# Second block of a two-block window-attention kernel: exponentials divided by their sums before they are turned, scores and mixes in one lump each, keys spread by transfers

## The chip, the cores and the metric

One core of a Trainium2 chip runs the whole program. The metric is the device time of one launch in microseconds (us). Every kernel computes in float32, with some products split into a high and a low part.

## The reference, cut to what matters

The input is 32 images of 56 x 56 pixels with 96 channels. Block 0 is a shifted 7 x 7 window attention with 12 heads of 8 channels and an MLP; the change doesn't touch it. Block 1 is this, with 8 x 8 windows and 6 heads of 16 channels:

```
xn = layernorm(x) * g1 + b1
windows = 8 x 8 windows of xn              # 32 * 49 = 1568 windows of 64 tokens
q, k, v = windows @ w_qkv + b_qkv          # 6 heads of 16; q is scaled by 1/4
attn = softmax(q @ k^T, axis=-1)           # exp(s - max) / sum, per query and head
out = attn @ v                             # per head
x = x + (out @ w_proj + b_proj)
h = gelu(layernorm(x) @ w_fc1 + b_fc1) @ w_fc2 + b_fc2    # 96 -> 384 -> 96
result = x + h
```

## The kernel before, in words

The program is two blocks one after the other, `swin_block` (names `swin_...` in the profile) and `plain_block` (names `plain_...`), with an array in DRAM between them. Only `plain_block` is changed.

It works in groups of 8 windows, which are 4 pairs (128 tokens each), so 196 groups. Nothing schedules the work but the order in which it is written: each engine has a `body(g, phase)` with a list of steps, and `run_groups` calls it for every `g`. A step carries an offset: `residual(-2, A)` in body `g` works on group `g - 2`. So a group passes through several bodies, and in each body the engines work on up to eight different groups. The main part is a hardware loop with 36 bodies in one turn. Steps are held together by counting semaphores, whose names are in the table `STEPS`; every step waits for its inputs and for the last reader of the buffer that it overwrites. The `x1` buffer is single, and so `residual` (VectorE, writes `x1`) waits for `x1_norm` and `x1_res` of the group before, both written by GpSimd.

What one group needs, with the engine:

- SyncE: four transfers of 48 KB load the windows (`load`, L1147), four store the result (`store`, L1154). A load may start when `x_res` and `x_norm` of two groups before are made.
- VectorE: mean and variance (`partial_x`, `moments_x`), GpSimd: their power -1/2, centring and scaling (`power_x`, `norm_x`), and `residual_x`, the input plus a constant row.
- TensorE turns the tokens (`turn_x`), ScalarE copies them twice (`copy_x`, `high_x`), and VectorE takes the difference of the two copies (`low_x`, L1505: both its inputs are in SBUF).
- TensorE makes keys, queries and values. VectorE adds the biases (`bias_k`, `bias_q`). GpSimd spreads the keys over two head columns by a multiplication with a 0/1 mask (`spread_keys`, L1548, two halves).
- TensorE: scores in two halves of two pairs (`scores`, L1195). VectorE: greatest score and difference (`shift`, once per pair). ScalarE: exponentials. TensorE turns them key-major (`turn_probs`), ScalarE copies them (`copy_turned`).
- TensorE: exponentials times values, and with a matrix of ones their sums, in two halves (`mix`, L1209). ScalarE: logarithm of the sums and exponential of its negative (`log_totals`, `invert_totals`). VectorE: product of the two (`normalise`).
- TensorE: projection. VectorE: first residual (`residual`), moments (`partial_x1`, `moments_x1`). GpSimd: `power_x1`, `norm_x1`, and `residual_x1` (writes `x1_res`). TensorE turns it, makes three chunks of the hidden layer (`hidden`), ScalarE GELU, TensorE `output`, VectorE `result`.

GpSimd's body before is:

```
residual_x(1); power_x(2); spread_keys(1, 0); spread_keys(1, 1)
norm_x(2); residual_x1(-2); power_x1(-2); norm_x1(-2)
```

Of the kernel before, what the change touches and what calls it, by code (L numbers as in the profile page):

```python
# [40 lines left out]
PAIRS = 4  # L41
# [15 lines left out]
class Plain:  # L57
# [18 lines left out]
    "reciprocal": "1 / sum of a group's first two pairs in the second block",  # L76
    "q_hat": "queries ready for the scores", "k_hat": "keys ready to be spread over heads",
    "k_heads": "two pairs' keys spread over heads",
# [3 lines left out]
    "prob": "exponentials",  # L82
# [879 lines left out]
def plain_block(nc, cfg, src, dst, par, const, psum):  # L962
# [14 lines left out]
    with ctx:  # L977

        def sb(name, shape, dtype=F32):
            return ctx.enter_context(nc.sbuf_tensor(f'{cfg.name}_{name}', shape, dtype))  # L980
# [22 lines left out]
        head_mask = sb('head_mask', [DIM, J])  # L1003
# [5 lines left out]
        sum_heads = sb('sum_heads', [128, HB, 32])  # L1009
# [15 lines left out]
        inv_total = sb('inv_total', [DIM, 2, 2 * TT])  # L1025
# [22 lines left out]
        with setup:  # L1048
# [13 lines left out]
            loads += [(ident[:, :], const['ident']), (w_fc1[:, :], par['fc1_w']), (w_fc2[:, :, :], par['fc2_w'].rearrange('(c p) n -> p c n', p=128)), (w_qkv[0:DIM, :], par['qkv_w']), (w_proj[0:DIM, :], par['proj_w']), (b_qk[:, :], par['qkv_b'][0:2 * DIM].rearrange('(t c) -> c t', t=2)), (b_v[:, :], column(par['qkv_b'][2 * DIM:3 * DIM])), (b_fc1[:, :], par['fc1_b'].rearrange('(c p) -> p c', p=128)), (row_fc2[:, :], every_row(par['fc2_b'], DIM)), (head_mask[:, :], const[f'{cfg.name}_head_mask']), (sum_heads[:, :, :], const[f'{cfg.name}_sum_heads'])]  # L1062
# [69 lines left out]
        def earlier_half(g, h):  # L1132
            return (g, 0) if h else (g - 1, 1)
        with nc.Block() as block:
# [4 lines left out]
            def _(sp):  # L1139
# [13 lines left out]

                def store(n, parity):  # L1154
# [4 lines left out]
                for n in range(8):  # L1159
                    load(n, n % 2)  # L1160
                with sp.Fori(4, groups // 2) as m:
# [3 lines left out]
                for n in range(groups, groups + 2):  # L1165
                    store(n - 8, n % 2)
# [6 lines left out]
            def _(pe):  # L1173

                def body(g, phase):
# [9 lines left out]
                    def all_windows(first):  # L1185
                        part, pair, column = [list(d) for d in first.ap]
                        return bass.AP(first.tensor, first.offset, [part, pair, [HALF, 2], column])

# [489 lines left out]
```

## Time and profile before

| | us |
|---|---|
| median of 3 runs | 7353.15 (7351.54 to 7354.21) |
| the profiled execution | 7355.68 |
| its span | 7353.9 |
| PE busy | 7179.3 (98%) |
| ACT busy | 6373.4 (87%) |
| DVE busy | 5991.6 (81%) |
| POOL busy | 5233.9 (71%) |

PE is TensorE, DVE is VectorE, ACT is ScalarE, POOL is GpSimd, and SPq is the queue on which SyncE issues transfers. The first block takes until about 4440 us of the span, the second the rest. A busy share is an average over the whole span: how much of it one group of the second block takes is read from the order of time.

### The profile page before, as it was taken

The page shows a single profiled execution, that of the slowest core. Times are in us where ns is not written, and L with a number is a line of the kernel's source. Part 1 is how long each engine was busy: PE and PEld are TensorE (multiplying, and loading weights), DVE is VectorE, ACT ScalarE, POOL GpSimd, SP SyncE. Part 2 cuts the span into 40 slices and gives each one's busy share as a digit, 9 for nine tenths or more (in the row PEclk, how much of TensorE's full clock was granted, in tenths as well). Part 3 has the DMA queues.
Part 4 walks back from the last instruction along what each step waited for, and adds up shares of the span by engine and source line. Part 5 has one row for each costly group of instructions (what it writes and reads, how often), then busy time and mean ns, then how long its engine had stood idle before and what let it go on. Part 6 is the DMA issues. An engine that isn't in the chain of part 4 may idle for free. (4 is left out here: it accounts for less than half of the span.)

```text
span 7353.9 us, 317113 instructions
## 1 busy us (share of the span) xinstructions
PE 7179.3 (98%) x113246; PEld 5509.1 (75%) x113246; DVE 5991.6 (81%) x12718; ACT 6373.4 (87%) x12032; POOL 5233.9 (71%) x5957
## 2 busy tenths in 40 slices
PE   6999999999999999999999996999999999999999
PEld 4777777777777777777777775777777777777777
DVE  5888888888888888888888885777777777777776
ACT  5999999999999999989999986887887887887887
POOL 3777777777777777777777775666666666666665
PEclk9999999999999999999999998999999999999999
DMA  0111111111111111111111101111111111111111
GB/s 21 30 30 30 29 30 30 29 29 31 30 30 29 30 30 30 29 29 30 29 30 29 30 25 24 30 30 29 30 30 29 30 30 29 30 30 29 30 30 26
DMA packets 342624, 214.39 MB, mean 29 GB/s; under 512 B 265624, under 2 KB 341144, under 8 KB 341144
## 3 DMA queue, kind: packets, MB, share of 16 engines
q1 hardware_dynamic: 341146, 194.49, 10.7%
q8 instruction: 951, 15.58, 0.9%
q14 instruction: 527, 4.32, 0.2%
HBM read 78.66 MB, written 77.07 MB: 21 GB/s over the span
## 5 line engine op out<-in xcount | busy, mean ns | idle before, releaser
L881 POOL TENSOR_TENSOR swin_score<-swin_score,swin_top 113x588 f32<-113x588 f32 x1024 | 1203.1, 1175 | 743.6 <-DVE swin_top L753 743.2
L624 ACT ACTIVATE swin_probT<-swin_ps_probs 128x339 f32<-128x339 f32 x2048 | 922.1, 450 | 199.2 <-PE swin_ps_probs L481 178.2
L1553 POOL TENSOR_TENSOR plain_k_heads<-plain_k_hat,plain_head_mask 96x512 f32<-96x512 f32 x392 | 398.9, 1037 | 897.1 <-DVE plain_k_hat L1444 897.1
L481 PE MATMUL swin_ps_probs<-swin_ident,swin_prob 113*128 113x113 f32 x6144 | 991.1, 270 | 7.0 <-ACT swin_probT L624 7.0
L481 PEld LDWEIGHTS swin_ps_probs<-swin_ident,swin_prob 113*128 113x128 f32 x6144 | 667.7, 141 | 355.6 <-issue 321.5
L748 DVE TENSOR_TENSOR swin_score<-swin_ps_scores,swin_bias_tab 113x588 f32<-113x588 f32 x1024 | 777.1, 759 | 174.1 <-PE swin_ps_scores L471 172.9
L753 DVE TENSOR_REDUCE swin_top<-swin_score 113x12 f32<-113x588 f32 x1024 | 769.0, 751 | 0.2
L630 ACT ACTIVATE swin_prob<-swin_score 113x588 f32<-113x588 f32 x1024 | 719.1, 702 | 5.8 <-POOL swin_score L881 2.9
L1431 DVE TENSOR_REDUCE plain_top<-plain_ps_scores 128x6 f32<-128x384 f32 x784 | 432.7, 552 | 263.0 <-PE plain_ps_scores L1206 263.0
L784 DVE SCALAR_TENSOR_TENSOR swin_x<-swin_y,swin_y_rstd,swin_x_res 98x96 f32<-98x96 f32 x1024 | 601.1, 644 | 0.8 <-POOL swin_y_rstd L899 0.7
L495 PEld LDWEIGHTS swin_ps_mixed<-swin_probT,swin_v_heads 128*32 128x32 f32 x24576 | 422.3, 109 | 222.2 <-issue 146.0
L471 PE MATMUL swin_ps_scores<-swin_k_heads,swin_q_hat 32*64 32x196 f32 (+1 forms) x12288 | 577.7, 347 | 4.8 <-DVE swin_score L748 4.8
L564 PE MATMUL swin_ps_dense<-swin_w_fc,swin_hid 128*98 128x96 f32 x6144 | 578.8, 251 | 1.2 <-ACT swin_hid L701 1.2
L1332 ACT ACTIVATE plain_probT<-plain_ps_probs 128x384 f32<-128x384 f32 x784 | 382.2, 488 | 221.1 <-PE plain_ps_probs L1230 220.9
L495 PE MATMUL swin_ps_mixed<-swin_probT,swin_v_heads 128*32 128x49 f32 x24576 | 563.0, 210 | 2.1 <-ACT swin_probT L624 1.0
L564 PEld LDWEIGHTS swin_ps_dense<-swin_w_fc,swin_hid 128*98 128x98 f32 x6144 | 560.8, 168 | 1.5 <-ACT swin_hid L701 1.5
L1271 PE MATMUL plain_ps_dense<-plain_w_fc,plain_hid 128*128 128x96 f32 x4704 | 554.2, 275 | 1.7 <-ACT plain_hid L1344 1.7
L1271 PEld LDWEIGHTS plain_ps_dense<-plain_w_fc,plain_hid 128*128 128x128 f32 x4704 | 542.6, 192 | 3.2 <-ACT plain_hid L1344 3.2
L1344 ACT ACTIVATE plain_hid<-plain_ps_dense,plain_b_fc 128x512 f32<-128x512 f32 x588 | 404.5, 688 | 148.7 <-PE plain_ps_dense L1183 130.8
L887 POOL TENSOR_TENSOR swin_x_res<-swin_x_in,swin_res_row 98x384 f32<-98x384 f32 x256 | 255.9, 1000 | 291.0 <-DVE swin_x L784 235.4
L1433 DVE TENSOR_TENSOR plain_score<-plain_ps_scores,plain_top 128x384 f32<-128x384 f32 x784 | 436.9, 557 | 27.0
L701 ACT ACTIVATE swin_hid<-swin_ps_dense,swin_b_fc 128x392 f32<-128x392 f32 x768 | 425.8, 589 | 7.5 <-PE swin_ps_dense L448 4.5
(187 smaller groups left out, 20907.6 us busy)
## 6 DMA issues: line engine op xcount, KB each, us to landing
swin_k_heads<-swin_k_hat SPq DMA_DIRECT2D x1024, 36.8 KB
plain_x_in<-between_blocks SPq DMA_DIRECT2D x784, 48.0 KB, 2.2
out_dram<-plain_x SPq DMA_DIRECT2D x784, 48.0 KB, 2.0
swin_x_in<-in_x SPq DMA_DIRECT2D x224, 136.5 KB
between_blocks<-swin_x SPq DMA_DIRECT2D x224, 136.5 KB
swin_x_in<-in_x SPq DMA_DIRECT2D x224, 19.5 KB
between_blocks<-swin_x SPq DMA_DIRECT2D x224, 19.5 KB
swin_x_in<-in_x SPq DMA_DIRECT2D x224, 2.6 KB
```

Source lines behind the costliest of these rows:

```text
L471: last = nc.tensor.matmul(psS[half * HALF:half * HALF + rows, band, 0:BC], q_hat[part, parity(d), w * WIN:w * WIN + rows], k_heads[part, p ...
L481: last = nc.tensor.transpose(psP[:, n * QT:(n + 1) * QT], prob[0:QT, p, 2 * hp:2 * hp + 2, :].rearrange('p h k -> p (h k)'), ident[0:QT, 0 ...
L495: last = nc.tensor.matmul(psO[32 * band:32 * band + 32, first:first + WIN], v_heads[:, (phase + d) % 4, 2 * p + half, band, n, :], probT[: ...
L564: last = nc.tensor.matmul(psM[0:TT, bank, p * DIM:(p + 1) * DIM], hid[:, c, p * TT:(p + 1) * TT], w_fc2[:, c, :], start=c == 0, stop=c == ...
L624: nc.scalar.activation(to, psP[:, 0:3 * QT], ACT.Copy).then_inc(did['probT'], 1)
L630: nc.scalar.activation(prob[0:QT, p, :, 0:WIN], score[0:QT, p % 2, :].rearrange('p (h k) -> p h k', k=WIN), ACT.Exp).then_inc(did['prob'], 1)
L748: nc.vector.tensor_tensor(score[0:QT, p % 2, :].rearrange('p (b n) -> p b n', b=BANDS), psS[0:QT, :, 0:BC], kind, ALU.add).then_inc(did['s ...
L753: nc.vector.tensor_reduce(top[0:QT, p % 2, :], score[0:QT, p % 2, :].rearrange('p (h k) -> p h k', k=WIN), AX.X, ALU.max).then_inc(did['to ...
L784: last = nc.vector.scalar_tensor_tensor(x1[:, p, :], y[:, p, :], y_rstd[:, p:p + 1], x_res[:, (phase + d) % 4, p, :], ALU.mult, ALU.add)
L881: nc.gpsimd.tensor_tensor(view, view, bcast(top[0:QT, p % 2, :], 2, WIN), ALU.subtract).then_inc(did['shifted'], 1)
L1271: last = nc.tensor.matmul(psM[0:TT, bank, p * DIM:(p + 1) * DIM], hid[:, c, p * TT:(p + 1) * TT], w_fc2[:, c, :], start=c == 0, stop=c == ...
L1433: nc.vector.tensor_tensor(shifted, from_psum, bcast(greatest, 3, WIN), ALU.subtract).then_inc(did['shifted'], 1)
```

## The change

In the second block:

- The exponentials are divided by their sums before they are turned. VectorE sums them per query and head, two pairs at a time, and takes the reciprocal (`total`); GpSimd multiplies (`scale_probs`, once per pair). `turn_probs` waits for `prob_scaled` in place of `prob`. The products with a matrix of ones, `log_totals`, `invert_totals` and `normalise` go; ScalarE copies the mixes to SBUF (`copy_mixed`).
- Scores of all four pairs are one lump of 24 products, and so are the mixes.
- The keys are spread by six SBUF-to-SBUF transfers from SyncE (`spread`), each of 16 rows of 512 numbers; `spread_keys` goes.
- The bodies of all engines are written in another order, some steps with another offset: GpSimd's steps on `x1` now work on group `g - 3` in place of `g - 2`, `output` and `result` on `g - 4`.

```diff
@@ SyncE
+                def spread(n, parity):
+                    sp.wait_ge(did['k_hat'], upto(n))
+                    sp.wait_ge(did['scored'], upto(n - 2, 1, 2))
+                    for band in range(BANDS):
+                        for j in range(J):
+                            rows = slice(32 * band + j * D, 32 * band + (j + 1) * D)
+                            sp.dma_start(k_heads[rows, parity, j, :], k_hat[rows, :]).then_inc(did['k_spread'], 16)
...
                         load(2 * m + k, k)
+                        spread(2 * m + k - 2, k)
                         store(2 * m + k - 8, k)
@@ TensorE
-                    def scores(d, h):
+                    def scores(d):
...
-                            pe.wait_ge(did['k_heads'], upto(g + d, h, 2))
-                            ug, uh = earlier_half(g + d, h)
-                            pe.wait_ge(did['shifted'], upto(ug, 2 * uh + 1, PAIRS))
-                            for p in (2 * h, 2 * h + 1):
+                            pe.wait_ge(did['k_spread'], spread_total(g + d))
+                            pe.wait_ge(did['shifted'], upto(g + d - 1, PAIRS - 1, PAIRS))
+                            for p in range(PAIRS):
...
-                            for band in range(BANDS):
-                                last = nc.tensor.matmul(psO[32 * band:32 * band + 32, SUMS:SUMS + 2 * TT], sum_heads[:, 0, :], all_windows(probT[:, 2 * h:2 * h + 2, band, 0:WIN]), start=True, stop=True)
...
-                            pe.wait_ge(did['prob'], upto(g + d, p, PAIRS))
+                            pe.wait_ge(did['prob_scaled'], upto(g + d, p, PAIRS))
@@ TensorE's body, without its waits for a free bank
-                    scores(0, 0); mix(-1, 0); keys(1, A); turn_probs(-1, 2); queries(1, B); project(-2, A); turn_probs(-1, 3)
-                    hidden(-3, 0, B); hidden(-3, 1, A); hidden(-3, 2, B); scores(0, 1); mix(-1, 1); values(1, A)
-                    turn_x(2); turn_probs(0, 0); output(-3, B); turn_x1(-2); turn_probs(0, 1)
+                    scores(0); keys(1, A); turn_probs(-1, 2); queries(1, B); turn_probs(-1, 3); turn_x(2); mix(-1)
+                    values(1, A); project(-2, B); turn_x1(-3); output(-4, A); hidden(-3, 0, B); turn_probs(0, 0)
+                    hidden(-3, 1, A); turn_probs(0, 1); hidden(-3, 2, B)
@@ ScalarE
-                            nc.scalar.activation(inv_total[:, h, :], psO[0:DIM, SUMS:SUMS + 2 * TT], ACT.Ln).then_inc(did['log_total'], 1)
...
-                            nc.scalar.activation(inv_total[:, h, :], inv_total[:, h, :], ACT.Exp, scale=-1.0).then_inc(did['inv_total'], 1)
+                    def copy_mixed(d):
...
+                            nc.scalar.activation(mixedT[0:DIM, parity(d), :], psO[0:DIM, 0:NT], ACT.Copy).then_inc(did['mixedT'], 1)
@@ VectorE
-                            nc.vector.tensor_tensor(mixedT[0:DIM, parity(d), 2 * h * TT:2 * (h + 1) * TT], psO[0:DIM, 0:2 * TT], inv_total[:, h, :], ALU.mult).then_inc(did['mixedT'], 1)
+                    def total(d, h):
+                        if exists(g + d, groups):
+                            dve.wait_ge(did['prob'], upto(g + d, 2 * h + 1, PAIRS))
+                            nc.vector.tensor_reduce(total_of[0:QT, h, :], prob[0:QT, 2 * h:2 * h + 2, :, 0:WIN].rearrange('q p h k -> q (p h) k'), AX.X, ALU.add).then_inc(did['total'], 1)
+                            dve.wait_ge(did['total'], upto(g + d, h, 2))
+                            dve.wait_ge(did['prob_scaled'], upto(g + d - 1, 2 * h + 1, PAIRS))
+                            nc.vector.reciprocal(inv_total[0:QT, h, :], total_of[0:QT, h, :]).then_inc(did['inv_total'], 1)
@@ GpSimd
-                            nc.gpsimd.tensor_tensor(k_heads[0:DIM, parity(d), :, tokens], bcast(k_hat[:, tokens], 1, J), bcast(head_mask[:, :], 2, 2 * TT), ALU.mult).then_inc(did['k_heads'], 1)
+                    def scale_probs(d, p):
+                        if exists(g + d, groups):
+                            pool.wait_ge(did['inv_total'], upto(g + d, p // 2, 2))
+                            pair = prob[0:QT, p, :, 0:WIN]
+                            nc.gpsimd.tensor_tensor(pair, pair, bcast(inv_total[0:QT, p // 2, p % 2 * heads:(p % 2 + 1) * heads], 2, WIN), ALU.mult).then_inc(did['prob_scaled'], 1)
```

The order on GpSimd (POOL) in one body of the steady part, before. `plain_x_norm` is the normalised input or x1, `plain_x_res` an input plus a constant row.

```order
L1537 TENSOR_TENSOR plain_x_res<-plain_x_in,plain_res_row 128x384 [waits plain_x1,plain_x_loaded_even]
L1543 TENSOR_TENSOR plain_var_eps<-plain_moments,plain_epsilon 128x4 [waits plain_rstd,plain_moments]
L1546 TENSOR_TENSOR plain_rstd<-plain_var_eps,plain_half_power 128x4 [waits plain_x_norm,plain_var_eps]
L1553 TENSOR_TENSOR plain_k_heads<-plain_k_hat,plain_head_mask 96x2x256 [waits plain_scored]
L1553 TENSOR_TENSOR plain_k_heads<-plain_k_hat,plain_head_mask 96x2x256 [waits plain_scored,plain_k_hat]
L1559 TENSOR_TENSOR plain_x_norm<-plain_x_in,plain_moments 128x384 [waits plain_x_turned,plain_moments]
L1562 TENSOR_TENSOR plain_x_norm<-plain_x_norm,plain_rstd 128x384 [waits plain_rstd,plain_x_centred]
L1568 TENSOR_TENSOR plain_x_res<-plain_x,plain_row_fc 128x384 [waits plain_x2,plain_x1]
L1574 TENSOR_TENSOR plain_var_eps<-plain_moments,plain_epsilon 128x4 [waits plain_rstd2,plain_moments2]
L1577 TENSOR_TENSOR plain_rstd<-plain_var_eps,plain_half_power 128x4 [waits plain_x1_norm,plain_var_eps2]
L1583 TENSOR_TENSOR plain_x_norm<-plain_x,plain_moments 128x384 [waits plain_x1_turned,plain_moments2]
L1586 TENSOR_TENSOR plain_x_norm<-plain_x_norm,plain_rstd 128x384 [waits plain_rstd2,plain_x1_centred]
```

The same body of GpSimd in the changed kernel (its lines are 7 to 16 lower).

```order
L1537 TENSOR_TENSOR plain_var_eps<-plain_moments,plain_epsilon 128x4 [waits plain_rstd,plain_moments]
L1540 TENSOR_TENSOR plain_rstd<-plain_var_eps,plain_half_power 128x4 [waits plain_x_norm,plain_var_eps]
L1552 TENSOR_TENSOR plain_x_norm<-plain_x_in,plain_moments 128x384 [waits plain_x_turned,plain_moments]
L1555 TENSOR_TENSOR plain_x_norm<-plain_x_norm,plain_rstd 128x384 [waits plain_rstd,plain_x_centred]
L1531 TENSOR_TENSOR plain_x_res<-plain_x_in,plain_res_row 128x384 [waits plain_x1,plain_x_loaded_even]
L1567 TENSOR_TENSOR plain_var_eps<-plain_moments,plain_epsilon 128x4 [waits plain_rstd2,plain_moments2]
L1570 TENSOR_TENSOR plain_rstd<-plain_var_eps,plain_half_power 128x4 [waits plain_x1_norm,plain_var_eps2]
L1576 TENSOR_TENSOR plain_x_norm<-plain_x,plain_moments 128x384 [waits plain_x1_turned,plain_moments2]
L1579 TENSOR_TENSOR plain_x_norm<-plain_x_norm,plain_rstd 128x384 [waits plain_rstd2,plain_x1_centred]
L1561 TENSOR_TENSOR plain_x_res<-plain_x,plain_row_fc 128x384 [waits plain_x2,plain_x1]
L1546 TENSOR_TENSOR plain_prob<-plain_prob,plain_inv_total 128x384 [waits plain_inv_total] x2
L1546 TENSOR_TENSOR plain_prob<-plain_prob,plain_inv_total 128x384 [waits plain_inv_total] x2
```

The write of `x1_res` (L1568 before, L1561 now) has moved from the third place behind the keys to the tenth, with all steps of `x_norm`, `x_res` and the `x1` moments ahead of it, and the four scalings follow.

VectorE (DVE) in the second half of a body before, from the last two `shift` to `result` of the next body.

```order
L1431 TENSOR_REDUCE plain_top<-plain_ps_scores 128x6 [waits plain_scored,plain_prob]
L1433 TENSOR_TENSOR plain_score<-plain_ps_scores,plain_top 128x384 [waits plain_top]
L1489 BN_STATS plain_stats<-plain_x_in 128x6 [waits plain_moments,plain_x_loaded_even]
L1489 BN_STATS plain_stats<-plain_x_in 128x6 x3
L1465 TENSOR_TENSOR plain_mixedT<-plain_ps_mixed,plain_inv_total 96x256 [waits plain_inv_total,plain_x_centred,plain_proj_made,plain_var_eps,plain_stats]
L1498 BN_AGGR plain_moments<-plain_stats 128x2 x4
L1505 TENSOR_TENSOR plain_xT_low<-plain_xT,plain_xT_high 96x512 [waits plain_q_made,plain_xT]
L1422 TENSOR_TENSOR plain_x<-plain_ps_dense,plain_x_res 128x384 [waits plain_x2_stored_even,plain_x1_res,plain_fc2_made]
```

VectorE in the changed kernel, from `residual` (L1451) to the end of the body.

```order
L1451 TENSOR_TENSOR plain_x<-plain_ps_dense,plain_x_res 128x384 [waits plain_x1_norm,plain_x1_res,plain_x_res,plain_proj_made]
L1456 TENSOR_REDUCE plain_total<-plain_prob 128x12 [waits plain_prob]
L1459 RECIPROCAL plain_inv_total<-plain_total 128x12 [waits plain_prob_scaled,plain_total]
L1430 TENSOR_TENSOR plain_x1T_low<-plain_ps_turn,plain_x1T_high 96x512 [waits plain_x1T]
L1466 BN_STATS plain_stats<-plain_x 128x6 [waits plain_moments2,plain_x1]
L1414 TENSOR_TENSOR plain_x<-plain_ps_dense,plain_x_res 128x384 [waits plain_fc2_made,plain_x1_res,plain_x1_centred,plain_x2_stored_even,plain_var_eps2,plain_stats2]
L1456 TENSOR_REDUCE plain_total<-plain_prob 128x12 [waits plain_prob]
L1459 RECIPROCAL plain_inv_total<-plain_total 128x12 [waits plain_prob_scaled,plain_total]
L1475 BN_AGGR plain_moments<-plain_stats 128x2 x4
L1483 BN_STATS plain_stats<-plain_x_in 128x6 x3
L1499 TENSOR_TENSOR plain_xT_low<-plain_xT,plain_xT_high 96x512 [waits plain_xT,plain_x_centred,plain_q_made,plain_var_eps,plain_stats]
L1492 BN_AGGR plain_moments<-plain_stats 128x2 x4
```

`xT_low` has moved ahead of the last four BN_AGGR, which make the `moments` that GpSimd's body begins with, and behind the second sum and reciprocal, which start two scalings on GpSimd.

## Rows read from the trace of the kernel before

**Rows 1.** Chain that ended last, 6000 to 6045 us: start, us, what.

```profile
6016.23 0.61 PE plain_ps_scores L1206 x24
...
6017.50 0.43 PE plain_ps_mixed L1221 x6
...
6021.92 0.70 ACT plain_hid L1344
...
6030.62 0.61 PE plain_ps_scores L1206 x24
```

**Rows 2.** One line of GpSimd, whole span: duration ns min/median/max, first and last start.

```profile
L1568 POOL TENSOR_TENSOR plain_x_res<-plain_x,plain_row_fc x196: 992/1000/1017, 4516.3 to 7332.0; 128x384 f32<-128x384 f32 x196
```

**Rows 3.** Order of time, POOL, 6016 to 6031 us: start, us, instruction, idle before it.

```profile
6019.84 2.03 POOL L1553 TENSOR_TENSOR plain_k_heads<-plain_k_hat,plain_head_mask 96x512 f32<-96x512 f32 x2 [4.54 <-DVE plain_k_hat L1444]
6021.83 0.83 POOL L1559 TENSOR_TENSOR plain_x_norm<-plain_x_in,plain_moments 128x384 f32<-128x384 f32 x1
...
6023.52 0.99 POOL L1568 TENSOR_TENSOR plain_x_res<-plain_x,plain_row_fc 128x384 f32<-128x384 f32 x1
6024.48 0.20 POOL L1574 TENSOR_TENSOR plain_var_eps<-plain_moments,plain_epsilon 128x4 f32<-128x4 f32 x1
...
6027.43 1.00 POOL L1537 TENSOR_TENSOR plain_x_res<-plain_x_in,plain_res_row 128x384 f32<-128x384 f32 x1
```

**Rows 4.** Order of time, DVE, 6016 to 6031 us.

```profile
6016.92 0.56 DVE L1431 TENSOR_REDUCE plain_top<-plain_ps_scores 128x6 f32<-128x384 f32 x1 [0.86 <-PE plain_ps_scores L1206]
6017.51 0.56 DVE L1433 TENSOR_TENSOR plain_score<-plain_ps_scores,plain_top 128x384 f32<-128x384 f32 x1
6017.99 0.68 DVE L1438 TENSOR_TENSOR plain_x1T_low<-plain_ps_turn,plain_x1T_high 96x512 fp32r<-96x512 f32 x1
6018.92 0.75 DVE L1444 TENSOR_SCALAR plain_k_hat<-plain_ps_dense,plain_b_qk 96x512 f32<-96x512 f32 x1 [0.25 <-PE plain_ps_dense L1183]
...
6022.42 0.73 DVE L1472 BATCH_NORM_STATS2 plain_stats<-plain_x 128x6 f32<-128x96 f32 x4
6023.18 0.42 DVE L1465 TENSOR_TENSOR plain_mixedT<-plain_ps_mixed,plain_inv_total 96x256 f32<-96x256 f32 x1
...
6029.16 0.69 DVE L1505 TENSOR_TENSOR plain_xT_low<-plain_xT,plain_xT_high 96x512 fp32r<-96x512 f32 x1 [1.20 <-ACT plain_xT_high L1383]
```

**Rows 5.** Order of time, start of the second block: VectorE hands moments to GpSimd.

```profile
4470.25 0.38 DVE L1498 BATCH_NORM_AGGREGATE plain_moments<-plain_stats 128x2 f32<-128x6 f32 x4
4470.71 0.20 POOL L1543 TENSOR_TENSOR plain_var_eps<-plain_moments,plain_epsilon 128x4 f32<-128x4 f32 x1 [18.39 <-DVE plain_moments L1498]
```

**Rows 6.** Groups by line, DVE, first block, 3000 to 4000 us: busy, mean ns.

```profile
L753 DVE TENSOR_REDUCE swin_top<-swin_score 113x12 f32<-113x588 f32 x237 | 178.0, 751 | 0.0
...
L799 DVE TENSOR_REDUCE swin_z_var<-swin_z_sq 98x4 f32<-98x384 f32 x59 | 31.8, 538 | 0.0
```

**Rows 7.** Groups by line, DVE, 0 to 60 us (set-up of the first block).

```profile
L314 DVE RECIPROCAL swin_inv_tau<-swin_inv_tau 96x1 f32<-96x1 f32 x1 | 0.2, 159 | 0.0
L313 DVE TENSOR_SCALAR swin_inv_tau<-swin_ps_dense 96x1 f32<-96x1 f32 x1 | 0.2, 153 | 0.0
```

**Rows 8.** Order of time, first block: POOL, then one instruction of DVE.

```profile
3010.38 1.00 POOL L943 TENSOR_TENSOR swin_x<-swin_z_ln,swin_x_res 98x384 f32<-98x384 f32 x1
3011.33 1.17 POOL L881 TENSOR_TENSOR swin_score<-swin_score,swin_top 113x588 f32<-113x588 f32 x1
...
3010.95 1.67 DVE L784 SCALAR_TENSOR_TENSOR swin_x<-swin_y,swin_y_rstd,swin_x_res 98x96 f32<-98x96 f32 x1
```

**Rows 9.** The same line of DVE, 2000 to 7000 us: duration ns min/median/max.

```profile
L784 DVE SCALAR_TENSOR_TENSOR swin_x<-swin_y,swin_y_rstd,swin_x_res x577: 302/305/2008, 1999.8 to 4421.6; 98x96 f32<-98x96 f32 x193
```

**Rows 10.** One line of SyncE, 2000 to 7000 us: keys spread in the first block.

```profile
L414 SPq DMA_DIRECT2D swin_k_heads<-swin_k_hat x564: 713/726/1602, 2007.6 to 4372.2; - x188
```

**Rows 11.** Order of time, SyncE's queue, 6027 to 6034 us.

```profile
6028.86 3.63 SPq L1152 DMA_DIRECT2D plain_x_in<-between_blocks  x4
```

**Rows 12.** The page, transfers: KB each, median us from issue to landing.

```profile
plain_x_in<-between_blocks SPq DMA_DIRECT2D x784, 48.0 KB, 2.2
```

More of the change, by code:

```diff
@@ L75 @@
     "sq_norm": "squared norms with their floor in SBUF", "log_norm": "their logarithm", "inv_norm": "1 / norm",
-    "reciprocal": "1 / sum of a group's first two pairs in the second block",
     "q_hat": "queries ready for the scores", "k_hat": "keys ready to be spread over heads",
-    "k_heads": "two pairs' keys spread over heads",
     "k_spread": "a head's keys of every band are in their own columns", "v_made": "values in dense bank 0", "v_heads": "... and in SBUF",
@@ L81 @@
     "top": "greatest score of each query and head", "shifted": "scores less their top",
-    "prob": "exponentials",
+    "prob": "exponentials", "total": "their sums, for two pairs", "prob_scaled": "exponentials times 1 / sum",
     "prob_turned": "exponentials turned in psP", "probT": "... and in SBUF",
@@ L1210, in mix @@
+                                if p % 2 == 1:
+                                    last.then_inc(did['scored'], 1)
+                    def mix(d):
                         if exists(g + d, groups):
                             pe.wait_ge(did['v_heads'], upto(g + d))
[L1212 to L1219 removed]
@@ L1220, in mix @@
-                            for band in range(BANDS):
-                                last = nc.tensor.matmul(psO[32 * band:32 * band + 32, SUMS:SUMS + 2 * TT], sum_heads[:, 0, :], all_windows(probT[:, 2 * h:2 * h + 2, band, 0:WIN]), start=True, stop=True)
+                            pe.wait_ge(did['probT'], upto(g + d, PAIRS - 1, PAIRS))
+                            pe.wait_ge(did['mixedT'], upto(g + d - 1))
+                            for w in range(WINDOWS):
+                                p, half = divmod(w, 2)
+                                for band in range(BANDS):
+                                    last = nc.tensor.matmul(psO[32 * band:32 * band + 32, w * WIN:(w + 1) * WIN], v_heads[:, parity(d), w, band, 0, :], probT[:, p, band, half * HALF:half * HALF + WIN], start=True, stop=True)
@@ L1305, in body @@
                     hidden(-3, 1, A)
-                    free(('hid', -3, 0, CHUNKS), ('q_hat', 1), ('x2', -4))
+                    turn_probs(0, 1)
+                    free(('hid', -3, 0, CHUNKS), ('x1', -2), ('q_hat', 1), ('hid', -4, 2, CHUNKS))
                     hidden(-3, 2, B)
-                    scores(0, 1)
-                    mix(-1, 1)
-                    free(('hid', -3, 1, CHUNKS), ('x1', -2), ('k_hat', 1), ('v_heads', 0))
-                    values(1, A)
-                    turn_x(2)
@@ L1586, in norm_x1 @@
                             nc.gpsimd.tensor_tensor(x1_norm[:, :, :], x1_norm[:, :, :], bcast(rstd2[:, :], 2, DIM), ALU.mult).then_inc(did['x1_norm'], 1)
+                    power_x(2)
+                    norm_x(2)
                     residual_x(1)
-                    power_x(2)
-                    spread_keys(1, 0)
-                    spread_keys(1, 1)
-                    norm_x(2)
-                    residual_x1(-2)
-                    power_x1(-2)
-                    norm_x1(-2)
+                    power_x1(-3)
+                    norm_x1(-3)
+                    residual_x1(-3)
+                    scale_probs(0, 0)
+                    scale_probs(0, 1)
+                    scale_probs(0, 2)
+                    scale_probs(0, 3)
                 run_groups(pool, groups, 36, body)
```

131 lines of the change are left out of this document (54 added, 77 removed).

## The prediction

> **What bounds the kernel now.** I read the chain of waits first. In the second block one body goes from one lump of scores to the same lump of the next body: 6016.23 to 6030.62, 14.39 us, and in all of it only one link is not TensorE, a GELU of 0.70 us that the third hidden chunk waits for [rows 1]. So TensorE's own work sets the pitch. Over the whole block the pitch is (7332.0 - 4516.3) / 195 = 14.44 us, which is 0.05 more than an undisturbed body, for the turns of the hardware loop and the like [rows 2]. The order of time of GpSimd comes next: it stands idle 4.54 us in each body until the keys are there [rows 3], so its chain of steps costs nothing today. VectorE also has waits (0.86, 0.25, 1.20 us) [rows 4]. The question is therefore not only what TensorE loses, but whether the new order ties GpSimd and VectorE into a ring that is longer than 14.39 us. A ring is what returns to the same step one body later; its length is a floor for the pitch.
>
> **What TensorE loses.** Per group, two sets of products with the matrix of ones go, 0.43 us each [rows 1]: 0.86 us. The other products stay in number and shape. TensorE's floor is 14.39 - 0.86 = 13.53 us, perhaps up to 0.3 less if the third hidden chunk no longer waits.
>
> **The new ring.** The diff and the order show it. GpSimd's body begins with power_x, which waits for `moments`, VectorE's last step of the body before. Then come norm_x, residual_x, power_x1, norm_x1 and, only now, residual_x1. VectorE's `residual` overwrites x1, so it waits for this `x1_res`. Behind `residual` VectorE has two sums, two reciprocals, low_x1, both sets of moments, result and low_x, and its last step makes the `moments` for GpSimd. Before, GpSimd's `x1` steps followed VectorE's `residual` in the same body (offset -2 on both), and no such ring closed.
>
> GpSimd's part, start to start [rows 3]: norm_x 6023.52 - 6021.83 = 1.69; a residual row 6024.48 - 6023.52 = 0.96; power and norm together 6027.43 - 6024.48 = 2.95, so power is 1.26; the last one counts in full, 1.00. Sum: 1.26 + 1.69 + 0.96 + 2.95 + 1.00 = 7.86 us.
>
> Hand-overs: the moments end at 4470.25 + 0.38 = 4470.63 and GpSimd starts at 4470.71: 0.08 [rows 5]. The way back is taken as the same.
>
> VectorE's part. Two instructions that don't depend on each other overlap by 0.08 (6017.51 + 0.56 against 6017.99); one that waits for the one before starts 0.03 behind its end (6016.92 + 0.56 against 6017.51) [rows 4].
> - residual and result: 0.56 - 0.08 = 0.48 each.
> - The sum over 768 exponentials isn't in the trace. Sums over 384 and 588 numbers in SBUF took 0.538 and 0.751 us [rows 6], which is 1.044 ns for each number more: 0.751 + 180 x 1.044 ns = 0.94. Bounds are 0.75 (the row of 588) and 1.08 (two of 384).
> - The reciprocal of 12 numbers isn't there either. Of one number it took 0.159 against 0.153 for a plain operation [rows 7]; if each number costs these 6 ns more, 12 cost 0.07: 0.23 in all. Bounds 0.16 and 0.40 (a cost per number three times that). The next instruction starts 0.06 before its end. Sum and reciprocal: 0.94 + 0.03 + 0.17 = 1.14, twice.
> - low_x1 0.60, low_x 0.61; four BN_STATS with the wait behind them 6023.18 - 6022.42 = 0.76, twice; BN_AGGR 0.30 in passing and 0.38 at the end [rows 4, 5].
>
> 0.48 + 1.14 + 0.60 + 0.76 + 0.48 + 1.14 + 0.30 + 0.76 + 0.61 + 0.38 = 6.65 us. The ring without collisions: 0.08 + 7.86 + 0.08 + 6.65 = 14.67 us.
>
> **The collision in the ring.** low_x has two inputs in SBUF. In the first block such an instruction with two inputs in SBUF, of 96 columns, takes 0.305 us in the median [rows 9], but 1.67 where it is sent at 3010.95 while GpSimd is in L943; it ends at 3012.62, that is 0.12 behind the end of the next instruction of GpSimd, L881 (3011.33 + 1.17 = 3012.50) [rows 8]. It stood still across both and ran only at their end: its free run would begin at 3012.62 - 0.305 = 3012.32, 0.18 before GpSimd's end; a little less, 0.15, is taken. Today low_x never meets that; in the order before it takes 0.69 [rows 4].
>
> In the new order it does. Count from the end of the second reciprocal. GpSimd starts two scalings at 0.08; a multiplication of 128x384 by a broadcast takes 0.83 (as L1559), 0.79 start to start: both end at 1.70. VectorE, from -0.06: BN_AGGR 0.30, BN_STATS 0.76, so low_x is sent at 1.00, inside the second scaling. It runs from 1.70 - 0.15 = 1.55: 0.55 us are lost, on the ring. Bounds: 0, if it isn't held, and 0.55 + 2 x 0.17 = 0.89, if a scaling takes 1.00 like L1568 [rows 3]. The row that is nearest says held, so I take 0.55.
>
> The rule of the Trainium skill, SBUF — State Buffer, section Who interferes with whom, speaks against this change: a VectorE instruction with two SBUF inputs and a GpSimd instruction that reads SBUF exclude each other, and the first one keeps the way for its whole length. By that low_x would start at 1.70 and lose 0.70, which as an estimate makes 29 us more than the sum below. The trace agrees that it is held, but shows it over two instructions and about 0.15 short of the end.
>
> **What lies beside.** VectorE's four shifts (4 x (0.59 + 0.48) = 4.28) and two biases (2 x 0.67) take 5.62 us after the moments, while x1_res comes at 0.08 + 7.86 + 0.08 = 8.02: `residual` waits 2.4 us, and this slack covers a late lump of scores. ScalarE loses four instructions on 96x256 and gets one copy of 96x512, at most 0.70 as the GELU of 128x512 [rows 1]; it gets lighter. TensorE has 13.5 of 15.2 us to do and waits for x_norm at turn_x.
>
> SyncE gets six transfers behind the four loads. The loads may start when x_res is made, 0.08 + 1.26 + 1.69 + 1.00 = 4.03 after the moments, and 0.43 later they do (6028.43 against 6028.86) [rows 3, 11]; they take 3.63, with 0.2 between lists 8.3. A transfer of keys in the first block, 24 rows, costs 0.726 of the queue [rows 10]; bounds for 16 rows are 0.48, if it goes by rows (16 of 24), and 3.63 / 4 = 0.91, a load of 128 rows [rows 11]. I take 0.73 with 0.05 between: 4.7, so issued by 13.0. With 2.2 to land, the landing of the 48 KB loads [rows 12], the keys are there at 15.2, just when the next body begins. The lump of scores needs some 1.3, and VectorE has 2.4 to spare, so up to 1.1 more costs nothing. The result's stores come behind and are waited for by nobody soon.
>
> **Sum.** Pitch 14.67 + 0.55 = 15.22, with 0.05 for the turns 15.27, against 14.44: 0.83 us x 196 groups = 163 us. At the end the MLP of the last group comes one body later; such an emptied body still has GpSimd's chain, up to 7.86 us: 8 us. 7355.7 (the profiled execution) + 163 + 8 = 7527; the median of the runs is 2.5 below the profiled one: 7524 us.
>
> **Rivals.**
> - *No collision.* low_x isn't held, or slips in front of the scaling. Pitch 14.67 + 0.05; (14.72 - 14.44) x 196 + 8 = 63: 7416 us. For it: low_x is sent only 0.13 after the second scaling starts. Against: [rows 8], where a gap between two GpSimd instructions didn't let the waiting one in. Chance 0.15.
> - *TensorE stays the bound* and the ring is shorter than I think: it decides if the ring is under 13.53. Then 0.86 x 196 = 169 less, 7184 us; with the sums at their lower bound and no collision the ring is 14.67 - 0.52 = 14.15, already (14.20 - 14.44) x 196 + 8 = -39: 7314 us. Against: GpSimd's 7.86 are measured one by one. Faster in all: 0.08; about the same 0.03.
> - *Keys too late.* From about 0.9 us per transfer the landing eats the slack. At 1.2 they are issued 2.8 later, 1.7 too late, and as the way from moments over x_res, loads and keys to scores comes back after two bodies, that is some 0.85 per group: 167 us more, 7691 us. Against: 0.726 for larger transfers. Chance 0.07.
>
> **How the numbers follow.** The forecast, ring with collision, has 0.62, with its own range 7460 to 7600. The rest, 0.05, is for longer terms (sum 1.08, reciprocal 0.40, scaling 1.00 together give 16.2 us). The range 7400 to 7600 takes in the rival without a collision and leaves out the faster cases, the late keys and the upper bounds, about 0.2. A difference of 0.2% (15 us) is what a measurement can tell. Slower 0.89, same 0.03, faster 0.08.
>
> **What would show it.** Right: GpSimd's power_x (L1537) waits for VectorE's BN_AGGR (L1492) in each body; `residual` (L1451) waits over 2 us for `x1_res` (L1561); low_x (L1499) takes about 1.2 us in place of 0.69; TensorE's busy share in the block is near 89%; the chain runs over POOL and DVE. Single terms: TENSOR_REDUCE L1456 0.94, RECIPROCAL L1459 0.23, scaling L1546 0.83, keys L1158 0.73. Wrong: a chain that is nearly all TensorE, low_x at 0.69, or scores that wait for SyncE's transfers.

## The result, and the profile after

| | before | after |
|---|---|---|
| device time, median of 4 runs each, us | 7352.34 | 7526.71 (7520.33 to 7536.2) |
| profiled execution, us | 7355.7 | 7536.2 |
| span, us | 7353.9 | 7534.4 |
| TensorE busy, 4600 us to shortly before the end | 98.8% (2668.11 of 2700.00) | 91.1% (2642.05 of 2900.00) |

The ratio is 1.0238 [1.0220, 1.0256]: 174 us slower, 2.4%. Forecast: 7524, range 7400 to 7600.

The page of the changed kernel, busy time and the share of the chain that ended last:

```profile
PE 7125.2 (95%) x110894; PEld 5485.8 (73%) x110894; DVE 6291.5 (84%) x13110; ACT 6293.5 (84%) x11444; POOL 5480.2 (73%) x6349
...
issue 20%; POOL 18%; PE 1%; POOLq 1%; DVE 0%; ACT 0%; SPq 0%; DMA 0%; ACTq 0%; DVEq 0%
```

The chain, which was TensorE's in [rows 1], now runs over GpSimd. The longest of its `issue` pieces (1.86, 1.25 and 0.88 us in a body) are the stretches in which GpSimd is idle and VectorE works, as the order of time and the waits below show. TensorE, the busiest engine over the whole span, is no longer full in the second block (91.1%). The lines of GpSimd's `residual_x1` and VectorE's low_x over the whole block (duration ns min/median/max, first and last start), to be held against [rows 2, 4]:

```profile
L1561 POOL TENSOR_TENSOR plain_x_res<-plain_x,plain_row_fc x196: 992/999/1011, 4535.1 to 7515.2; 128x384 f32<-128x384 f32 x196
L1499 DVE TENSOR_TENSOR plain_xT_low<-plain_xT,plain_xT_high x196: 689/1351/1356, 4471.9 to 7461.3; 96x512 fp32r<-96x512 f32 x196
```

The pitch is (7515.2 - 4535.1) / 195 = 15.28 us against 14.44, and low_x takes 1.35 us in place of 0.69. Now VectorE in order of time (start, us, instruction, idle before it), from one `residual` to the next; the answer to [rows 4]:

```profile
6015.90 0.56 DVE L1451 TENSOR_TENSOR plain_x<-plain_ps_dense,plain_x_res 128x384 f32<-128x384 f32 x1 [2.49 <-POOL plain_x_res L1561]
6016.37 0.94 DVE L1456 TENSOR_REDUCE plain_total<-plain_prob 128x12 f32<-128x768 f32 x1
6017.35 0.23 DVE L1459 RECIPROCAL plain_inv_total<-plain_total 128x12 f32<-128x12 f32 x1
6017.49 0.62 DVE L1430 TENSOR_TENSOR plain_x1T_low<-plain_ps_turn,plain_x1T_high 96x512 fp32r<-96x512 f32 x1
...
6020.62 0.71 DVE L1483 BATCH_NORM_STATS2 plain_stats<-plain_x_in 128x6 f32<-128x96 f32 x4
6021.36 1.35 DVE L1499 TENSOR_TENSOR plain_xT_low<-plain_xT,plain_xT_high 96x512 fp32r<-96x512 f32 x1
6022.64 0.37 DVE L1492 BATCH_NORM_AGGREGATE plain_moments<-plain_stats 128x2 f32<-128x6 f32 x4
...
6031.10 0.56 DVE L1451 TENSOR_TENSOR plain_x<-plain_ps_dense,plain_x_res 128x384 f32<-128x384 f32 x1 [2.53 <-POOL plain_x_res L1561]
```

And GpSimd beside it, the answer to [rows 3]:

```profile
6017.65 1.61 POOL L1546 TENSOR_TENSOR plain_prob<-plain_prob,plain_inv_total 128x384 f32<-128x384 f32 x2 [1.89 <-DVE plain_inv_total L1459]
6020.55 1.62 POOL L1546 TENSOR_TENSOR plain_prob<-plain_prob,plain_inv_total 128x384 f32<-128x384 f32 x2 [1.28 <-DVE plain_inv_total L1459]
6023.08 0.20 POOL L1537 TENSOR_TENSOR plain_var_eps<-plain_moments,plain_epsilon 128x4 f32<-128x4 f32 x1 [0.92 <-DVE plain_moments L1492]
...
6029.96 1.00 POOL L1561 TENSOR_TENSOR plain_x_res<-plain_x,plain_row_fc 128x384 f32<-128x384 f32 x1
```

The ring can be walked here. VectorE from `residual` to the end of the moments: 6023.01 - 6015.90 = 7.11. Hand-over 0.07. GpSimd from 6023.08 to 6030.96: 7.88. Hand-over 0.14. Sum 15.20, the distance from one `residual` to the next. The four pieces follow one another, so they must add up to it; what the walk shows is that nothing but these two engines stands on the way. low_x is sent at 6021.36, inside the second scaling; its last 0.69 us begin at 6022.71 - 0.69 = 6022.02, that is 0.15 before the scaling ends at 6022.17. It stood 0.66 us. It was a close meeting: that scaling starts at 6021.34, 0.02 before low_x is sent.

The waits of 5000 to 7000 us (total, times, longest):

```profile
POOL plain_prob L1546 <- DVE plain_inv_total L1459: 435.7, 260, 6.5
DVE plain_x L1451 <- POOL plain_x_res L1561: 311.4, 126, 2.6
...
POOL plain_var_eps L1537 <- DVE plain_moments L1492: 120.2, 130, 1.3
```

GpSimd waits for VectorE and VectorE for GpSimd, each in every body: the mark of a ring between two engines of which neither is full.

### The profile page after: what moved, and what is told of

Same layout as the page of the kernel before. It is cut to its first block and busy times, and to the rows that moved or that the text cites. A ratio compares the mean times of both kernels' runs of the same rounds, so it can differ in the third digit from the quotient of the medians.

```text
span 7534.4 us, 313308 instructions
## 1 busy us (share of the span) xinstructions
PE 7125.2 (95%) x110894; PEld 5485.8 (73%) x110894; DVE 6291.5 (84%) x13110; ACT 6293.5 (84%) x11444; POOL 5480.2 (73%) x6349
## 5 line engine op out<-in xcount | busy, mean ns | idle before, releaser
L1546 POOL TENSOR_TENSOR plain_prob<-plain_prob,plain_inv_total 128x384 f32<-128x384 f32 x784 | 635.0, 831 | 671.6 <-DVE plain_inv_total L1459 671.6
L1451 DVE TENSOR_TENSOR plain_x<-plain_ps_dense,plain_x_res 128x384 f32<-128x384 f32 x196 | 109.2, 557 | 487.3 <-POOL plain_x_res L1561 458.9
```

Of the source, the lines that this page charges most:

```text
L1546: nc.gpsimd.tensor_tensor(pair, pair, bcast(inv_total[0:QT, p // 2, p % 2 * heads:(p % 2 + 1) * heads], 2, WIN), ALU.mult).then_inc(did['p ...
```

## The experiments

Pitches are, as in [rows 2], the distance of the first and last start of GpSimd's `residual_x1` over 195. Ratios are to the kernel before on the same chip, with 95% intervals; the first four runs share one set of runs of before (7355.21), the next four another (7353.12), the last two a third (7353.27).

| run | us | ratio | pitch |
|---|---|---|---|
| e1_lowx_last | 7426.85 | 1.0095 [1.0078, 1.0112] | 14.76 |
| e2_two_x1 | 7462.99 | 1.0144 [1.0127, 1.0161] | 14.93 |
| e2b_two_x1_lowx_last | 7372.93 | 1.0026 [1.0015, 1.0037] | 14.49 |
| e3_x1res_first | 7546.28 | 1.0261 [1.0244, 1.0278] | 15.36 |
| e4_lowx_early | 7462.02 | 1.0147 [1.0130, 1.0164] | 14.92 |
| e5_keys_gpsimd | 7526.06 | 1.0234 [1.0217, 1.0251] | 15.26 |
| e7_keys_twice | 7999.69 | 1.0881 [1.0863, 1.0899] | 17.65 |
| e8_before_no_ones | 7207.74 | 0.9802 [0.9786, 0.9818] | 13.69 |
| e9_new_order | 7222.93 | 0.9825 [0.9809, 0.9841] | 13.71 |
| e10_new_order_two_x1 | 7223.09 | 0.9824 [0.9808, 0.9841] | 13.72 |

**low_x behind the moments.**

```diff
                     partial_x(3)
-                    low_x(2)
                     moments_x(3)
+                    low_x(2)
```

(and a one-column tensor_scalar ahead of the moments, 0.15 us, here and wherever the moments follow their statistics at once)

> The changed kernel with low_x moved behind the last four BN_AGGR, so that GpSimd's moments no longer wait for it; in front of these BN_AGGR stands one operation on a single number, about 0.06 us. Theory A (the ring of GpSimd and VectorE, with low_x held by the scalings): the ring loses 0.61 of low_x and 0.66 of its hold. Then the longer way is the one through the scalings: from residual to the second reciprocal's end 4.57, scalings 0.08 + 1.58, GpSimd's six steps 7.88, way back 0.14: 14.25 us a body, 0.95 less than now, 7341 us. Theory B (TensorE waits for late lumps: scores of four pairs and keys by transfers): low_x isn't on the way, so 7527 us within 0.2%. Theory C (low_x is on the ring but isn't held, it is only slow): 7527 - 196 x 0.61 or more, that is 7407 us if only its free length counts.

Measured: 7426.85, 100 us faster than after. low_x left the ring, but the gain was 0.52 us a group and not the 0.95 of theory A. VectorE and GpSimd at that place:

```profile
6009.44 0.99 DVE L1502 TENSOR_TENSOR plain_xT_low<-plain_xT,plain_xT_high 96x512 fp32r<-96x512 f32 x1
```

```profile
6008.27 1.61 POOL L1549 TENSOR_TENSOR plain_prob<-plain_prob,plain_inv_total 128x384 f32<-128x384 f32 x2 [1.28 <-DVE plain_inv_total L1461]
6009.85 0.65 POOL L1540 TENSOR_TENSOR plain_var_eps<-plain_moments,plain_epsilon 128x4 f32<-128x4 f32 x1
```

low_x was held 0.30 by the end of the scaling (free run from 10.43 - 0.69 = 9.74; the scaling ends at 9.88), and then GpSimd's small addition, which takes 0.20 alone, was held 0.45 by low_x (it ends 0.07 behind it). The ring is 14.25 + 0.45 = 14.70; from one `residual` to the next it measured 14.68. The hold goes both ways, and moving low_x handed 0.45 of the price to the other engine.

**x1 in two buffers, alone and with low_x last.**

```diff
-        x1 = sb('x1', [TT, PAIRS, DIM])
+        x1 = sb('x1', [TT, 2, PAIRS, DIM])
 ...
-                            dve.wait_ge(did['x1_res'], upto(g + d - 1))
+                            dve.wait_ge(did['x1_res'], upto(g + d - 2))
```

> The changed kernel with two buffers for x1, so that residual waits for x1_norm and x1_res of two groups before. Theory A: the ring through residual is cut. What is left is the ring turn_x1, output, result, second sum, moments, GpSimd up to norm_x1, with low_x still held, about 14.4 us a body: 7527 - 0.8 x 196 = 7370 us; residual then waits for TensorE's projection, not for GpSimd. Theory B (late lumps): x1's buffer has no part, no change within 0.2%. Theory D (VectorE has simply too much work): no change within 0.5%.

> Both: two buffers for x1, and low_x behind the last BN_AGGR. Theory A: both rings are now under TensorE's own work, 13.46 us a body, so the 0.86 us that TensorE lost come out at last: 7527 - 1.74 x 196 = 7186 us, 2.3% under the kernel before. Theory B: 7527, or at best what one of the two alone gave. Theory D (VectorE's work, 12.5 us of 15.2, is the bound): not under 7350.

Measured: 7462.99 and 7372.93, both faster than after and both far short of the expectation, by about 0.5 and 0.9 us a group. `residual` no longer waits for GpSimd; what it waits for instead stands in the second run's trace, VectorE (its L1453 is `residual`, L1416 `result`):

```profile
6002.96 0.56 DVE L1453 TENSOR_TENSOR plain_x<-plain_ps_dense,plain_x_res 128x384 f32<-128x384 f32 x1 [0.77 <-PE plain_ps_dense L1261]
...
6006.64 0.56 DVE L1416 TENSOR_TENSOR plain_x<-plain_ps_dense,plain_x_res 128x384 f32<-128x384 f32 x1 [0.82 <-PE plain_ps_dense L1275]
6007.12 0.94 DVE L1458 TENSOR_REDUCE plain_total<-plain_prob 128x12 f32<-128x768 f32 x1
```

A second ring lay under the first: x_norm (GpSimd), turn_x, mix, values, project, turn_x1, output (TensorE, one behind the other), `result` (VectorE), and behind `result`, only because VectorE runs in order, the second sum, the scalings, power_x and x_norm again. TensorE waits 0.34 us in it, at turn_x:

```profile
6013.48 0.64 PE L1284 MATMUL plain_ps_turn<-plain_ident,plain_x_norm 128*96 128x128 f32 x4 [0.34 <-POOL plain_x_norm L1558]
```

The expectation for the first run had named `result` and the second sum, but had taken them on to `moments` and x1_norm and counted 14.4; the one for the second run had put both rings under TensorE's own work. Neither had walked the way through x_norm and TensorE's steps behind turn_x. The second sum doesn't need `result`: this pointed to the order of the last two runs.

**GpSimd's residual_x1 first.** The call moves from the end of GpSimd's x1 steps to the head of its body.

> The changed kernel with residual_x1 as GpSimd's first step in a body, in the 0.92 us in which GpSimd waits for moments, in place of the step behind norm_x1. The ring loses its 1.00 us. Theory A with a hold over all instructions that GpSimd runs one behind the other (as the first block's rows showed): low_x now waits for the second scaling and for this step as well, 0.96 more, and all is lost again: 15.3 us a body, 7530 to 7550 us, low_x about 2.3 us long. Theory A' (the hold lasts for the one instruction that GpSimd is in): low_x stays at 1.35 us and the pitch falls to 14.3, 7350 us. Theory B: 7527.

Measured: 7546.28, as theory A said in time, but the trace doesn't bear out its reason, and so the agreement is luck. low_x took 1.35 us and not 2.3: it didn't wait for a second instruction. Its free run began 0.15 before the scaling's end (8.14 against 8.29), and it held the next one:

```profile
6007.48 1.35 DVE L1499 TENSOR_TENSOR plain_xT_low<-plain_xT,plain_xT_high 96x512 fp32r<-96x512 f32 x1
```

```profile
6006.67 1.62 POOL L1546 TENSOR_TENSOR plain_prob<-plain_prob,plain_inv_total 128x384 f32<-128x384 f32 x2 [1.83 <-DVE plain_inv_total L1459]
6008.24 1.45 POOL L1561 TENSOR_TENSOR plain_x_res<-plain_x,plain_row_fc 128x384 f32<-128x384 f32 x1
```

1.45 in place of 1.00: the same 0.45 as in the first run. This hold alone doesn't make up for the 1.00 that the ring lost. The rest stands at `result`, which now waits for TensorE's `output`:

```profile
6004.91 0.56 DVE L1414 TENSOR_TENSOR plain_x<-plain_ps_dense,plain_x_res 128x384 f32<-128x384 f32 x1 [0.59 <-PE plain_ps_dense L1273]
```

The walk, from `residual` at 6001.46 to the next at 6016.77: VectorE to the end of the moments 7.66 (7.11 in after), then 0.54 until GpSimd is free of `residual_x1` (0.07), GpSimd to the end of x1_norm 6.92 (7.88), back 0.19 (0.14). Sum 15.31, against 15.20. Theory A', 7350 us, was right about the length of the hold on low_x and wrong in time, by these two waits that it left out. A hold across two instructions of GpSimd, which I had read out of [rows 8], is not what happens in the second block; why L784 stood through both there stays open.

**low_x ahead of the second sum.**

> The changed kernel with low_x in front of the second sum: still on the ring, but at a time when GpSimd has finished the first two scalings and the last two haven't begun; one operation on a single number stands in front of the last BN_AGGR. Theory A: low_x takes 0.69 in place of 1.35. The way that then is longest is the one through the scalings, 14.25 + 0.61 = 14.86 us a body, 0.34 less than now: 7460 us. If the long low_x isn't a collision but its own cost, it stays at 1.35 and the time rises to about 7590 us (low_x 1.35 on the way through the scalings).

Measured: 7462.02, one body 14.84, as theory A said; low_x takes 0.68 here, so its 1.35 in after isn't a cost of its own. It starts as the first two scalings end (6011.23), and GpSimd then idles until the second reciprocal: no hold arises. The 65 us to after, 0.37 of pitch, aren't the price of the hold alone, since the longest way now runs over low_x, the second sum and the scalings. From the rows of after, the ring without the hold would be 15.20 - 0.66 = 14.54; that is an estimate, and no run took only the hold away.

```profile
6011.22 0.68 DVE L1502 TENSOR_TENSOR plain_xT_low<-plain_xT,plain_xT_high 96x512 fp32r<-96x512 f32 x1
```

**Keys by GpSimd again, everything else as after.** The two multiplications with `head_mask` stand ahead of the first scaling, and SyncE's transfers go.

> The changed kernel with the keys spread by GpSimd's two multiplications as before, behind residual_x1, and without the six transfers a group. Theory A: GpSimd waits 1.9 us for the first reciprocal at that place, so the 2.03 us fit almost, and the ring isn't touched: 15.2 to 15.3 us a body, 7520 to 7550 us. Theory B (keys by transfers come late): 7527 minus what the transfers cost, clearly less, down to TensorE's 13.5 us a body, 7200 us.

Measured: 7526.06, as after within its spread. The transfers are no cause: without them the pitch is 15.26 against 15.28. The 2.04 us of multiplications go into the time in which GpSimd waited for the first reciprocal.

**Twelve transfers of keys per group**, six of them to a buffer that nobody reads.

> The changed kernel with every transfer of keys issued twice, the first time to a buffer that nobody reads: twelve in place of six. The six take 3.77 us of SyncE's queue, so the keys land 3.8 us later. Theory A: they land now just when the next lump of scores may start; VectorE has 2.5 us to spare in front of residual. Of 3.8 us some 1.3 are left over, and the way from moments over loads and keys to scores comes back after two bodies: 0.6 to 0.8 us a body, 7640 to 7680 us. Theory B (keys are the bound already): 3.8 us in every second body at least, 1.9 a body: 7900 us. If the transfers aren't near the critical way at all: 7527.

Measured: 7999.69, above both theories (7640 to 7680, and 7900). The rows of SyncE's transfers and TensorE's waits for them (5000 to 7000 us), and the clock over 4600 to 7900 us (PEclk is the third number from the end):

```profile
L1160 SPq DMA_DIRECT2D plain_k_heads<-plain_k_hat x1176: 579/589/1757, 4478.0 to 7939.9; - x196
```

```profile
PE plain_ps_scores L1213 <- DMA plain_k_heads<-plain_k_hat: 242.5, 92, 6.1
```

```profile
4600.00:7900.00 3300.00, 2810.05 (x36233) 2262.81 (x36230) 2320.82 (x6309) 2095.36 (x3528) 2007.16 (x2602) 0.88 0.21 46
```

Each issue still takes 0.59 us, but twelve of them with loads and stores fill 7.5 + 3.6 + 3.6 = 14.7 of SyncE's body, and the scores wait up to 6.1 us. TensorE's granted clock falls to 0.88 in this stretch, where it was 0.99 in after; it had idled in these waits just before. After the long wait the lump of scores took 2.00 us, after a short one 1.12:

```profile
6011.20 2.00 PE L1213 MATMUL plain_ps_scores<-plain_k_heads,plain_q_hat 32*64 32x128 f32 x48 [3.48 <-DMA plain_k_heads<-plain_k_hat]
6028.03 1.12 PE L1213 MATMUL plain_ps_scores<-plain_k_heads,plain_q_hat 32*64 32x128 f32 x48 [0.60 <-DMA plain_k_heads<-plain_k_hat]
```

The two aren't taken apart by this run. It shows that the rival "keys too late" was real as a mechanism with 3.8 us more of queue time; how much less would do isn't shown.

**The kernel before without its products with ones in the second block.** Its sums are set to 1 once, so it leaves out part of the computation.

> The kernel before, without the products with the matrix of ones in the second block (the sums are then a constant 1 that is put there once; logarithm, exponential and product stay). This is what TensorE loses in the change, alone. If TensorE's own work sets the pitch of the kernel before, each group gets 0.86 us shorter: 7352 - 169 = 7183 us. If another engine is close behind, less: ScalarE works 12.9 us in a body, so at 14.39 - 0.86 = 13.53 it has little room; 7200 to 7250 us then.

Measured: 7207.74, pitch 14.44 - 13.69 = 0.75 shorter. So the term 0.86 was worth 0.75, 145 us in all. TensorE is still the bound there (busy 2467.16 of 2500.00 us); where the other 0.11 went stays open.

**A new order on VectorE, with one x1 buffer and with two.**

```diff
                     residual(-2, B)
                     total(0, 0)
                     low_x1(-3)
-                    partial_x1(-2)
-                    result(-4, A)
                     total(0, 1)
-                    moments_x1(-2)
+                    result(-4, A)
                     partial_x(3)
-                    low_x(2)
                     moments_x(3)
+                    partial_x1(-2)
+                    low_x(2)
+                    moments_x1(-2)
```

> What changes: only VectorE's order behind the residual of the changed kernel: residual, first sum, low_x1, second sum, result, BN_STATS and moments of x (with the tiny filler), BN_STATS of x1, low_x, moments of x1. So nothing but low_x1 (0.54) stands between the two sums. Traces of the runs so far: with low_x last GpSimd's addition of epsilon took 0.65 instead of 0.20, so each ring so far has carried a hold of 0.45 on one engine or the other. Theory R (the ring over both sums is what is long, and it can be cut by order alone): VectorE 0.48 + 1.12 + 0.54 + 1.12 = 3.26, hand-over 0.08, two scalings 1.58, GpSimd's rest 7.85 with perhaps 0.45 of hold, hand-over 0.14: 12.9 to 13.4 for that ring; moments of x are ready about 1.7 us behind the second reciprocal, as the scalings end. Then TensorE decides: in the run with two x1 buffers and low_x last it waited only 0.34 for x_norm and some 0.4 for probT in a turn of 14.35, so 13.5 to 13.8 a group and 7190 to 7260 us. Theory S (it is TensorE's chain turn_x, mixed, values, project, output to VectorE's result that decides, as the two-buffer runs suggest, and moving the sum off it helps only a little): 14.1 to 14.3, 7310 to 7350.

> The new order and x1 in two buffers. Theory R: TensorE is the bound in both, so the same as the new order alone within 10 us (7190 to 7260). If the ring over the residual still decided with one buffer, this run is faster than the other by more than 20 us.

Measured: 7222.93 and 7223.09, 304 us faster than after and 130 us (1.75%) faster than before; theory R, both inside its range. The second buffer is worth nothing once the order is right. Lumps of scores and keys by transfers stay as in after, so they aren't what made it slower. Before `residual` VectorE now waits for TensorE, in 195 of 196 bodies (for GpSimd once, 4.2 us), and GpSimd scales all four pairs in one go:

```profile
L1453 DVE TENSOR_TENSOR plain_x<-plain_ps_dense,plain_x_res x196: 557/558/559, 4516.4 to 7195.8; 128x384 f32<-128x384 f32 x196
...
  PE plain_ps_dense L1261: 129.2, 195
```

```profile
5999.96 3.28 POOL L1549 TENSOR_TENSOR plain_prob<-plain_prob,plain_inv_total 128x384 f32<-128x384 f32 x4 [2.45 <-DVE plain_inv_total L1461]
6003.20 0.20 POOL L1540 TENSOR_TENSOR plain_var_eps<-plain_moments,plain_epsilon 128x4 f32<-128x4 f32 x1
6003.48 1.02 POOL L1543 TENSOR_TENSOR plain_rstd<-plain_var_eps,plain_half_power 128x4 f32<-128x4 f32 x1
...
6013.52 3.28 POOL L1549 TENSOR_TENSOR plain_prob<-plain_prob,plain_inv_total 128x384 f32<-128x384 f32 x4 [2.46 <-DVE plain_inv_total L1461]
```

One body is 13.56 us, and TensorE is busy 2415.07 of 2500.00 us (96.6%). low_x now falls beside GpSimd's power:

```profile
6003.76 0.69 DVE L1502 TENSOR_TENSOR plain_xT_low<-plain_xT,plain_xT_high 96x512 fp32r<-96x512 f32 x1
```

It lies wholly inside L1543 (6003.48 to 6004.50), and both take what they take alone. The run changes the place of several steps at once, so it doesn't say what each of them is worth.

## Why the prediction was right

- *TensorE's loss of work, 0.86.* Mis-sized a little: 0.75 by the run without the products. It decided nothing in the changed kernel, since TensorE was no longer the bound (busy 91.1% where near 89% was forecast).
- *The ring as the new bound.* Shown: low_x out of the ring, x1 in two buffers, and the new order each shorten the time, and the new order brings the pitch to 13.71, next to the 13.69 that the kernel before has without the products. The signs named in advance came: power_x waits for the moments, `residual` 2.49 us for `x1_res`, low_x takes 1.35.
- *GpSimd 7.86, hand-overs 0.08 and 0.08.* 7.88, 0.07 and 0.14. The way back is longer than the way there, 0.06 that I had taken as equal.
- *VectorE 6.65 without the collision.* 7.11 - 0.66 = 6.45. The sum (0.94), the reciprocal (0.23) and the scaling (0.83) came out as taken; each pair of sum and reciprocal takes 1.12 start to start where 1.14 was taken, low_x1 0.54 for 0.60, BN_AGGR in passing 0.23 for 0.30. 0.20 too long in all, the rest in hundredths.
- *The collision 0.55.* 0.66: low_x is sent 0.89 behind the second reciprocal's end (6020.47 to 6021.36) and not 1.00, into the same scaling, which ends at 1.70 as forecast. So 0.11 of the 0.20 comes back as hold, and that is no luck: what VectorE saves between the reciprocal and low_x, the hold takes again. 7.20 forecast, 7.11 measured. The rival without a collision was nearer than the prediction had it: low_x is sent 0.02 behind the start of the second scaling and not 0.13. It was held all the same, in the median of all 196 bodies; what a slightly earlier low_x does isn't shown. That it is held was the choice of the prediction, and low_x (1.35 against 0.69 when alone, and 0.68 where its place is moved) shows it. The row that I took it from led me to think that a waiting instruction doesn't get in between two of GpSimd's. In this kernel it would have made no difference, as nothing stood behind the scaling; in the trace of the run with `residual_x1` first it is wrong.
- *The Trainium skill, SBUF — State Buffer, section Who interferes with whom.* That the two exclude each other agrees with every collision shown above, in both directions. As to the whole length, the traces show a little less: the free run of the one that is held begins 0.13 to 0.15 us before the end of the other. One case goes against it, GpSimd's power, which has two SBUF inputs too: it doesn't hold a low_x that is sent while it runs (0.69 inside its 1.02, in the new order). The other way round it is held, as at one place of the kernel before:

```profile
4521.30 0.69 DVE L1505 TENSOR_TENSOR plain_xT_low<-plain_xT,plain_xT_high 96x512 fp32r<-96x512 f32 x1 [1.03 <-ACT plain_xT_high L1383]
4521.49 1.38 POOL L1546 TENSOR_TENSOR plain_rstd<-plain_var_eps,plain_half_power 128x4 f32<-128x4 f32 x1
```

- *The pitch.* 15.22 forecast and 15.20 measured for a body; 15.27 and 15.28 as a mean. That it is this near owes something to errors that cancel by luck: 0.09 too much on VectorE, 0.02 too little on GpSimd and 0.05 on the hand-overs.
- *The ends, 8 us.* The first `residual_x1` is 4535.1 - 4516.3 = 18.8 us later, and from the last one to the span's end it is 19.2 instead of 21.9 us: 16 us in all. Filling and emptying the longer pipeline costs more than I had counted. The 8 us that are missing don't show in the median: of the four runs of after the profiled one is the slowest, 9.5 us above the median, where 2.5 was taken off. The profiled execution was forecast at 7527 and took 7536; that 7524 comes so near to 7526.71 is luck.
- *Keys.* 0.59 an issue in place of 0.73, 2.0 to land in place of 2.2: less than taken, and the scores' wait for them is 31.5 us in 41 of 196 bodies over the block. Taking the transfers away changed nothing.
- *The rivals.* Without a collision 7416 was forecast; it didn't occur in after, and no run took only the hold away. The run with low_x early is the nearest, 7462, and the one with low_x last, 7427, still had 0.45 of it on the other engine. TensorE as the bound, 7184, wasn't what after did, but the new order with the same work came to 7223.

## What to carry to other kernels

Where a change makes two engines wait for each other in both directions, add up the ring start to start before counting what any engine saves; its length, not a busy share, is the new floor, and work that merely stands in an engine's order inside the ring counts as much as work that belongs to it. A better order was worth more here than a second buffer: with two x1 buffers and low_x last 7373 us, with the new order 7223, with one buffer or two. The sum in front of an unrelated wait is one part of that order; its share wasn't measured. Before expecting a gain from breaking one ring, look for the next one, through every engine that takes part.

## What the runs showed of the hardware

- low_x, with two inputs in SBUF, and GpSimd's additions and multiplications out of SBUF exclude each other both ways: low_x 1.35 instead of 0.69 behind a scaling, and GpSimd's next instruction 0.65 instead of 0.20, or 1.45 instead of 1.00, behind low_x. The loser runs from about 0.14 us before the winner's end.
- low_x1, one of whose two inputs is in PSUM, wasn't held: 0.62 us beside the scalings of after, 0.68 before, when GpSimd was idle [rows 3, 4].
- low_x sent during GpSimd's power (128x4) ran without any loss to either, 0.69 and 1.02. The power sent 0.19 behind low_x took 1.38.
- A transfer of 16 rows of keys within SBUF costs 0.59 us of SyncE's queue and lands 2.0 us behind its issue.
- A reciprocal of 12 numbers a row took 0.23 us, a sum of 768 numbers 0.94.
